# Expanding a rank-three state: fp32 product of three rows, or bfloat16 product of twenty-seven rows

## The reference

```
counts = segment_sum(ones, seg_ids); pooled = segment_sum(x, seg_ids)   # seg_ids are all 0
h = pooled / max(counts, 1)                                           # only row 0 is not zero
prop(z) = segment_sum(edge_weight * z[src], dst)
for i in range(5):
    z = h @ W[i] + b[i]
    x_start = prop(z); xi = h
    for _ in range(5):
        xi = (prop(xi) + x_start) / 2.9
    h = leaky_relu(batch_norm(xi))
return h[seg_ids]
```

## Time and profile before

| | us |
|---|---|
| median of 3 runs | 9455.91 (9445.86 to 9458.88) |
| the profiled execution's own time | 9455.72 |
| its span in the profile | 9453.9 |
| inner layer 0, first scalar copy to the last copy of the expansion | 986.9 to 1754.1 |
| expansion, 50 groups | 1582.4 to 1754.1 |

### The profile page before, as it was taken

One profiled execution on the slowest core, in us unless ns is written; L12 is line 12 of the kernel. 1 busy time (PEld: TensorE's weight loads), 2 busy tenths in 40 slices (PEclk: granted clock), 3 DMA queues, 4 the chain that ended last, 5 costly groups with the idle time before them and its releaser, 6 DMA issues. The chain is left out here.

```text
span 9453.9 us, 109668 instructions
## 1 busy us (share of the span) xinstructions
PE 5807.2 (61%) x24229; PEld 4281.7 (45%) x24229; DVE 4952.6 (52%) x12073; ACT 2449.6 (26%) x6228; POOL 6665.9 (71%) x6509
## 2 busy tenths in 40 slices
PE   4646556777775677765777765777751676730190
PEld 2436223555554555554555544555541565630170
DVE  5669665563334753335743345633347675630277
ACT  0116000222224222224222233222236112630006
POOL 4767674477777777777777777777777677977566
PEclk8765786775555765555855556855555787975555
DMA  3127101566664766654766666666656223631118
GB/s 146 43 89 264 29 2 26 110 119 100 101 104 98 129 111 99 101 100 103 137 102 101 101 100 115 124 101 105 101 100 226 83 67 119 248 125 29 20 32 330
DMA packets 472142, 1025.40 MB, mean 108 GB/s; under 512 B 146139, under 2 KB 179724, under 8 KB 471396
## 3 DMA queue, kind: packets, MB, share of 16 engines
q0 software_dynamic: 192032, 330.70, 29.6%
q1 hardware_dynamic: 262212, 589.56, 17.4%
q10 hardware_dynamic: 17664, 102.61, 2.6%
HBM read 562.28 MB, written 472.47 MB: 109 GB/s over the span
## 5 line engine op out<-in xcount | busy, mean ns | idle before, releaser
L1018 POOL DMA_INDIRECT G<-tab,gidx x4000 | 3960.3, 990 | 1617.0 <-issue 1408.4
L1365 PE MATMUL PS<-M,G 128*128 128x128 f32 x6400 | 2257.8, 476 | 1299.6 <-DMA G<-tab,gidx 902.2
L1365 PEld LDWEIGHTS PS<-M,G 128*128 128x128 f32 x6400 | 1549.4, 311 | 2032.7 <-DMA G<-tab,gidx 1451.9
L1313 ACT ACTIVATE M<-ident,wz 128x128 f32<-128x128 f32 x3200 | 1021.5, 390 | 2376.5 <-DVE UO L1421 1223.8
L1421 DVE TENSOR_TENSOR_SCAN UO<-keyrow,UT,PS 128x512 f32<-128x512 f32 (+1 forms) x400 | 511.8, 1279 | 1290.5 <-PE PS L1365 1290.5
L1421 DVE TENSOR_TENSOR_SCAN UT<-keyrow,UO,PS 128x512 f32<-128x512 f32 (+1 forms) x400 | 511.8, 1279 | 1190.4 <-PE PS L1365 1190.4
L758 ACT ACTIVATE big<-big,nb,rs 128x128 f32<-128x128 f32 x1173 | 461.3, 480 | 426.7 <-POOL nb L749 360.3
L1105 POOL DMA_INDIRECT Y<-pair_d,G x400 | 402.7, 1007 | 199.8 <-issue 130.6
L1443 DVE TENSOR_TENSOR Y<-PS,big 128x512 f32<-128x512 f32 x800 | 535.9, 670 | 14.0 <-PE PS L1390 7.5
L1390 PE MATMUL PS<-ident,UT 128*128 128x128 f32 x1600 | 422.5, 419 | 8.3 <-DVE UT L1421 8.3
L1390 PE MATMUL PS<-ident,UO 128*128 128x128 f32 x1600 | 423.1, 420 | 0.0
(11 more groups left out here) (500 smaller groups left out, 11173.4 us busy)
## 6 DMA issues: line engine op xcount, KB each, us to landing
tab<-Y SPq DMA_DIRECT2D x1050, 256.0 KB, 2.8
big<-agg SPq DMA_DIRECT2D x90, 832.0 KB, 8.2
G<-tab,gidx POOLq DMA_INDIRECT x4000, 3.8
WR<-w_d SPq DMA_DIRECT2D x200, 256.0 KB
big<-x SPq DMA_DIRECT2D x60, 832.0 KB, 4.9
xt_d<-big SPq DMA_DIRECT2D x30, 884.0 KB, 3.6
x2n<-big ACTq DMA_DIRECT2D x30, 838.5 KB, 3.5
big<-x2n SPq DMA_DIRECT2D x30, 838.5 KB, 5.4
```

What stands on the lines that cost most here:

```text
L1018: pool.indirect_dma_start(G[:, t % RG, 0:D], None, tab_in(k), bass.IndirectOffsetOnAxis(ap=gidx[:, t:t + 1], axis=0)).then_inc(l_got[t % R ...
L1313: ins = nc.scalar.activation(M[:, GR * h + j, :], ident[:], ACT.Copy, scale=wz[:, bass.ds((NB * i + q) * GR + j, 1)])
L1365: ins = nc.tensor.matmul(PS[:, FT_[h], j, :], G[:, s, 0:D], M[:, GR * h + j, :], start=True, stop=True)
```

## The change

The three coefficient arrays and the three fixed rows are each split into three bfloat16 parts whose sum is the fp32 value (cast, cast back, subtract, twice, and a last cast). The product of a coefficient and a row is then the sum of nine products of parts, and with three pairs of operands the contraction is over 27 rows. The coefficient parts go to a DRAM tensor `coef_b` of 27 rows in which row 9b + 3a + k has part a of array k, for each b; the parts of the fixed rows go through DRAM (`rows_d`) into `R27`, in which row 9b + 3a + k has part b of row k. Each group then loads 27 x 512 in bfloat16, and the five products have 27 rows of bfloat16 in place of 3 rows of fp32. The work of the evacuating engines and the stores of the table stay as they were.

```diff
-        coef_d = dram("coef_d", (3, T * P))
+        coef_d = dram("coef_d", (T * P,))
+        coef_b = dram("coef_b", (27, T * P), BF16)
+        rows_d = dram("rows_d", (9, D), BF16)
...
+        CB = [flatY[0:TG, 384 * a:384 * a + 384].bitcast(BF16).rearrange("p (k g i) -> p k g i", k=3, g=2) for a in range(3)]
+        R3 = flatY[0:TG, 1152:1152 + 768].rearrange("p (k g i) -> p k g i", k=3, g=2)
+        H3 = flatG[0:TG, 1800:1800 + 768].rearrange("p (k g i) -> p k g i", k=3, g=2)
+        RP = WR[0:3, 0, 256:448].bitcast(BF16).rearrange("p (b f) -> p b f", b=3)
+        R27 = WR[0:27, 1, 256:320].bitcast(BF16)
+        RR, RH = (WR[0:3, k, 256:384] for k in (2, 3))
+        def C27(g):
+            return WR[0:27, g % NG, 0:256].bitcast(BF16)
+        def coefficient_parts(eng, b):
+            for a in range(3):
+                for k in range(3):
+                    eng.dma_start(coef_b[9 * b + 3 * a + k, :].rearrange("(g t i) -> t g i", g=2, i=P),
+                                  CB[a][:, k, :, :]).then_inc(o_cs, 16)
+        def split(dve, parts, value, back):
+            for a, part in enumerate(parts):
+                link(dve, "dve", nc.vector.tensor_copy(part, value))
+                if a < 2:
+                    link(dve, "dve", nc.vector.tensor_copy(back, part))
+                    link(dve, "dve", nc.vector.tensor_tensor(value, value, back, ALU.subtract))
...
         def scalars_sp(sp):
...
+            sp.wait_ge(l_rows, 2)
+            sp.dma_start(rows_d.rearrange("(b k) f -> k b f", k=3), RP).then_inc(o_rp, 16)
+            sp.wait_ge(o_rp, 16)
+            for b in range(3):
+                for a in range(3):
+                    sp.dma_start(R27[9 * b + 3 * a:9 * b + 3 * a + 3, :], rows_d[3 * b:3 * b + 3, :]).then_inc(o_rp, 16)
             for r in range(1, SR):
...
-            sp.wait_ge(o_co, 1)
-            for k, v in enumerate((A5, SAD[:, 0, :, :], SAD[:, 1, :, :])):
-                sp.dma_start(coef_d[k, :].rearrange("(g t i) -> t g i", g=2, i=P), v).then_inc(o_cs, 16)
-            sp.wait_ge(o_cs, 48)
+            sp.wait_ge(o_cb, 1)
+            for b in range(2):
+                coefficient_parts(sp, b)
+            sp.wait_ge(o_cs, 16 * 27)
             def coefficient_rows(g):
-                sp.dma_start(WR[0:3, g % NG, :], coef_d[0:3, GR * g * P:GR * (g + 1) * P]).then_inc(o_cf[g % NG], 16)
+                sp.dma_start(C27(g), coef_b[:, GR * g * P:GR * (g + 1) * P]).then_inc(o_cf[g % NG], 16)
...
             nc.vector.tensor_copy(A5, AB[:, :, :, 0]).then_inc(o_co, 1)
+            link(dve, "dve", nc.vector.tensor_copy(R3[:, 0, :, :], AB[:, :, :, 0]))
+            link(dve, "dve", nc.vector.tensor_copy(R3[:, 1:3, :, :].rearrange("p k g i -> p (k g i)"),
+                                                   SAD.rearrange("p k g i -> p (k g i)")))
+            split(dve, CB, R3, H3)
+            nc.vector.memset(col[:, 5:6], 0.0).then_inc(o_cb, 1)
             dve.wait_ge(o_c3, 1)
...
+            pe.wait_ge(o_rp, 160)
             for g in range(GPR):
-                c = WR[0:3, g % NG, :]
+                c = C27(g)
...
-                nc.tensor.matmul(bank(g % 2), rows4[0:3, 0:D], c, start=True, stop=True)
+                nc.tensor.matmul(bank(g % 2), R27, c, start=True, stop=True)
                 for j in range(GR):
-                    ins = nc.tensor.matmul(PS[:, 2 + g % 2, j, :], c[:, P * j:P * j + P], rows4[0:3, 0:D],
+                    ins = nc.tensor.matmul(PS[:, 2 + g % 2, j, :], c[:, P * j:P * j + P], R27,
...
         def scalars_act(act):
+            act.wait_ge(o_cb, 1)
+            coefficient_parts(act, 2)
...
+                        dve.wait_ge(l_rows, 1)
+                        link(dve, "dve", nc.vector.tensor_copy(RR, rows4[0:3, 0:D]))
+                        split(dve, [RP[:, b, :] for b in range(3)], RR, RH)
+                        nc.vector.memset(col[:, 5:6], 0.0).then_inc(l_rows, 1)
                         scalars_dve(dve)
```

More of the change, by code:

```diff
@@ L227, in _ @@
                 sp.wait_ge(s_cf, 1)
-                for row, v in ((coef_d[0, :], FA), (q_d, FB), (w_d, VB)):
+                for row, v in ((coef_d, FA), (q_d, FB), (w_d, VB)):
                     sp.dma_start(row.rearrange("(g t i) -> t g i", g=2, i=P), v).then_inc(s_cs, 16)
@@ L1062, in build @@
         (o_ld, o_ab, o_st, o_idx, o_got, o_hi, o_h8, o_hr, o_oh, o_ct, o_tb, o_pg, o_tt, o_v, o_vt, o_tl, o_cr,
-         o_co, o_cs, o_c3, o_sm, o_ex, o_rt, o_rd, o_en) = (
-            sem("o_" + n) for n in ("ld ab st idx got hi h8 hr oh ct tb pg tt v vt tl cr co cs c3 sm ex rt rd en").split())
+         o_co, o_cs, o_c3, o_sm, o_ex, o_rt, o_rd, o_en, o_rp, o_cb) = (
+            sem("o_" + n) for n in ("ld ab st idx got hi h8 hr oh ct tb pg tt v vt tl cr co cs c3 sm ex rt rd en rp cb").split())
         o_cf = sems("o_cf", NG)
         SR = NL - 1
+        CB = [flatY[0:TG, 384 * a:384 * a + 384].bitcast(BF16).rearrange("p (k g i) -> p k g i", k=3, g=2) for a in range(3)]
[17 more added lines that the diff above has]
+                    link(dve, "dve", nc.vector.tensor_tensor(value, value, back, ALU.subtract))
         def scalars_sp(sp):
-            for k, row in enumerate((coef_d[0, :], q_d)):
+            for k, row in enumerate((coef_d, q_d)):
                 sp.dma_start(SAD[:, k, :, :], row.rearrange("(g t i) -> t g i", g=2, i=P)).then_inc(o_ld, 16)
```

## The result

The changed kernel takes 9346.42 us (median of 4 runs, 9333.0 to 9352.74) against 9451.85 (4 runs, 9445.86 to 9458.88) on the same chip: ratio 0.9887, 95% interval 0.9875 to 0.9898, some 105 us less. A second comparison on another chip gave 0.9876 (0.9859 to 0.9892).

What follows compares the result with a forecast made beforehand. TensorE's products were taken to bound the expansion, at columns times passes and 1.2 GHz. From 9455.7 us, minus 119.2 (expansion), plus 12.9 (later first product), plus 2.4 (row split), gave 9351.8 us; range 9335 to 9385.

Steps and rivals of the forecast that it cites:

- rival E: Expansion products: a 27-row product takes the fp32 product's time, group stays at 3.41 us, total 9471 us; chance 0.02.
- The price of a group: Expansion: one group's five products, weight loads back to back with columns under them, set the pitch at 1.03 us.
- rival C: Expansion's short products: weight loads don't hide behind columns, 1.46 us a group, total 9373 us; chance 0.1.
- The hand-over of two pairs of banks: Expansion: products, VectorE's copy and signals over two groups take 1.91 us, 0.96 a group, under the products' 1.03.
- The loop of the coefficient ring: Expansion: coefficient loads issued five groups ahead need a pitch over 0.81 us, under the products' 1.03.
- Rival A: Expansion: 27 rows bring clock 1.0 (2.4 GHz), pitch 0.82 to 0.87 us, total 9343 us; chance 0.2.
- The split of the coefficients: Preparation after the copy of `A5`: copies, casts and subtractions on the path take 5.9 us.
- The stores: Preparation: 27 coefficient stores, 540 packets on each of ten engines at 22.5 ns, 12.2 us, 13.4 with latencies.
- Rival B: Coefficient stores: each 256-byte packet costs 58 ns, 31.3 us in place of 12.2, total 9371 us; chance 0.11.
- Rival D: Coefficient stores: their ring blocks SyncE, 9.93 us a store, 179 us in place of 12.2, total 9519; chance 0.02.
- The first product: Start of the expansion: first product comes 12.9 us later, at 1595.3, within 8.3 to 23 us.
- The split of the rows: Before the first gather of the scalars: small operations on the fixed rows, all on the path, add 2.4 us.

## Why the prediction was right

The total was forecast at 9351.8 and measured at 9346.4; the gain 104 us, measured 105. The mechanism was right; that the two gains agree to 1 us is luck. The stage itself changed by 110.4 us in the trace: the expansion gained 3 us more and the preparation cost 3 us less than forecast, and the rest of the distance to 105 is the spread of stages that the change does not touch.

- **What bounds the stage** held: columns times passes. Three rows of bfloat16 run at 0.94 us a group and 27 rows of fp32 at 3.41, so type and not rows made the gain. This also settles rival E, which said that a 27-row product would take the fp32 time: the five products of a group follow at 0.85 us, which is their 1024 columns at 1.2 GHz in one pass.
- **The price of a group**, 1.03 us forecast, 0.973 measured, is the term whose reasoning failed while its size came out near, by luck. The weight loads behind the short products cost nothing (0.107 us a product, the lower bound of that step; rival C is out), and 0.85 us would be the pitch if products set it. They don't: two loops do that the prediction had worked out and set aside as smaller. The hand-over of two pairs of banks, priced at 0.96, is 0.94: 1.04 us from a product's start to its copy (1602.27 to 1603.31), 0.69 and 0.15, over two groups. The loop of the coefficient ring, priced at 0.81, is products 1.0, copy 0.73, store issue 0.41, and 2.0 to 2.45 us from a load's issue to the product (issues at 1605.17 and 1606.78, products at 1607.15 and 1609.23), 4.1 to 4.6 us over five groups, 0.83 to 0.92 a group, plus SyncE's own queue, whose two issues take 0.82 us a group when it is behind. It gets behind by a long issue, as the store of 1.09 us at 1604.03, which the prediction left out; the first wait for a load in the expansion, 0.36 us at 1607.12, is for the load issued right behind it. With either loop lifted alone, or nearly, a group takes 0.943 (3 rows, light loads) or 0.955 (four pairs of banks); with both lifted 0.853. Rival A had the pitch at 0.82 to 0.87 once the clock is up; at a clock of 0.94 the ring held it at 0.922.
- **The split of the coefficients**: 5.9 us forecast, 5.8 measured; casts between fp32 and bfloat16 cost what fp32 copies do per element, in either direction (0.29 us for 256, 0.43 for 512 in copies, 0.56 for 768 in casts).
- **The stores**: 13.4 us forecast, 10.2 measured. The step was mis-sized by its packet price, 22.5 ns, and so 12.2 us of packets where 9.2 were measured (slices 4 to 39). The price was laid between a burst of ten 128-byte packets, 19 ns each, and one of sixty 512-byte packets, 29 ns each. Ten packets are mostly start and end: by the share of the queue a 128-byte packet occupies its engine for 13 ns, and one of 256 bytes for 18. That the engines alone set the time was not quite so: SyncE's 18 issues took 8.82 us, not 7.6, and end nearly with the packets. Rival B, double price for pieces under 512 bytes, is out. By the Trainium skill ("DMA: Bandwidth & Descriptors", Specifications) a transfer of under 512 bytes is read, modified and written and misses the line rate. The trace agrees in direction only, with 18 ns for 256 bytes against 28 for 512, somewhat over a quarter more per byte. Rival D is out too: SyncE's longest store issue was 0.75 us.
- **The first product**, 12.9 us later forecast, 9.9 measured, follows from that.
- **The split of the rows**: 2.4 forecast, 2.2 measured, and on the path, as moving it showed.
- **The clock** stayed at 1.2 GHz, as the forecast had it against rival A. Its reason was incomplete: unbroken work of few rows does not bring 2.4 GHz, but unbroken work of 128 rows does. What the rival was right in is that rows matter; 27 were not enough. The Trainium skill ("TensorE: Matmul & The Clock Gate", Part 1) ties the clock to how busy the engine has been. This case doesn't agree with that alone: two kernels with equally busy records, 171.06 of 171.6 and 90.18 of 90.9 us, were granted 0.50 and 0.97.

## What to carry to other kernels

When a stage is bound by TensorE and the granted clock is 0.50 although the engine never pauses, look at how many rows its products use: padding 3 rows to 128, zeros in one operand, halved such a stage, for a memset. Where TensorE no longer holds the stage, as in the changed kernel, the same padding gave 0.05 us a group. Splitting fp32 into bfloat16 parts on the contraction's spare rows did the same products in one pass where fp32 took four, and then the next limits were a factor of three and a half away, not ten. Price the hand-over of banks as a loop over their pairs, and the ring of operand loads as a loop over its depth, with the issuing engine's own backlog in it. When two such loops lie close together, lifting one shows next to nothing (0.02 us here) and lifting both shows what they cost (0.12): an experiment that lifts one alone does not acquit it. A gain of 5 us in a 9300 us kernel has to be read from its stage, since the total can't show it.

## What the runs showed of the hardware that was not expected

- The granted clock followed the rows: 0.50 with 3 and with 27 rows (fp32 and bfloat16), 0.97 with 128 rows of fp32, 0.94 with 128 of bfloat16, the last with TensorE busy only 31 of 46 us.
- Four products of 128 columns, each with a weight load of its own of 27 x 128 in bfloat16, start 0.108 us apart at 1.2 GHz; the loads are free.
- A packet of 256 bytes, from SBUF to DRAM, occupied its engine for 18 ns, one of 512 bytes for 28 and one of 128 bytes for 13.
- A load of 27 rows that reads 9 rows three times by a stride of zero took SyncE 0.70 us to issue, in place of 0.36, and kept one to three tenths of the 16 engines at work at a time.
- The first gather behind the table stores began 3.1 to 3.2 us after the last copy in some executions and 4.6 to 5.3 in others, of the changed kernel too.
